# Expert outputs scattered with addition into four rows per token, in a four-part sequence kernel

## The reference

```
logits = x @ gate_w.T ; scores = softmax(logits)          # 64 experts
topk_w, topk_idx = top_k(scores, 6)                       # six experts per token
# an expert takes its first 64 tokens (CAP); the rest is dropped
g = silu(buf @ w_gate) ; u = buf @ w_up ; d = (g * u) @ w_down
y[t] = sum over the experts that took t of  topk_w * d
y = y + shared feed-forward of x
```

## Time and profile before

| what | value |
|---|---|
| time, median of 3 runs | 695.05 us (693.71 to 695.93) |
| the profiled execution: its time, and its span | 695.07 us, 693.3 us |
| TensorE, VectorE, ScalarE, GpSimd busy | 85%, 74%, 28%, 15% |
| chain of waits by engine | PE 50%, DVE 33%, DMA 6%, issue 4%, ACT 3% |
| HBM read, written | 83.99 MB, 30.15 MB |

### The profile page before, as it was taken

One profiled execution on the slowest core, in us unless ns is written; L12 is line 12 of the kernel. 1 busy time (PEld: TensorE's weight loads), 2 busy tenths in 40 slices (PEclk: granted clock), 3 DMA queues, 4 the chain that ended last, 5 costly groups with the idle time before them and its releaser, 6 DMA issues.

```text
span 693.3 us, 7285 instructions
## 1 busy us (share of the span) xinstructions
PE 589.8 (85%) x2297; PEld 334.7 (48%) x2297; DVE 514.0 (74%) x1126; ACT 192.2 (28%) x375; POOL 106.4 (15%) x120
## 2 busy tenths in 40 slices
PE   7569999789998859987889958949599799999865
PEld 6444565435555346543455513534287344444454
DVE  7989888068895859999689996899978355555355
ACT  1112231136432344322543305413110223323000
POOL 2022020300002000020000030000000456664200
PEclk9889999899999959999799977979899999999999
DMA  7960000419102291010750014993071299996497
GB/s 278 405 208 25 16 32 0 134 66 352 43 0 69 93 353 51 23 38 1 282 182 24 1 38 154 348 333 129 0 251 38 77 330 367 373 374 240 178 413 296
DMA packets 50036, 114.62 MB, mean 165 GB/s; under 512 B 6096, under 2 KB 32464, under 8 KB 49488
## 3 DMA queue, kind: packets, MB, share of 16 engines
q1 hardware_dynamic: 42064, 94.36, 38.0%
q0 software_dynamic: 5632, 17.70, 7.3%
q10 hardware_dynamic: 2304, 2.10, 0.9%
HBM read 83.99 MB, written 30.15 MB: 165 GB/s over the span
## 4 chain that ended last, share of the span: by engine, by line
PE 50%; DVE 33%; DMA 6%; issue 4%; ACT 3%; SPq 2%; POOL 1%; DVEq 0%; POOLq 0%; ACTq 0%
PE gate_ps L712 7%; DVE scan_area L1315 7%; PE gate_ps L841 6%; PE up_ps L712 6%; PE misc_ps L729 5%; DMA bc<-part_rows 4%; DVE scan_area L1311 3%; DVE scan_area L1318 3%; PE turn_ps L652 3%; PE ssm_ps L671 3%; PE ssm_ps L761 3%; PE ssm_ps L859 3%; PE misc_ps L812 3%; PE misc_ps L859 3%; SPq L563 2%
## 5 line engine op out<-in xcount | busy, mean ns | idle before, releaser
L1315 DVE TENSOR_TENSOR_SCAN scan_area<-scan_area 128x1024 f32<-128x1024 f32 x32 | 73.3, 2292 | 4.4 <-ACT scan_area L999 0.9
L712 PE MATMUL gate_ps<-big,front_area 128*128 x144 | 74.8, 645 | 1.4 <-ACT front_area L899 1.4
L761 PE MATMUL ssm_ps<-scan_area,ident 128*128 128x512 f32 x128 | 63.5, 629 | 12.6 <-DVE scan_area L1318 11.9
L712 PE MATMUL up_ps<-big,front_area 128*128 x144 | 70.1, 610 | 0.0
L729 PE MATMUL misc_ps<-big,front_area 128*128 x288 | 65.6, 381 | 4.2 <-ACT front_area L899 3.8
L729 PEld LDWEIGHTS misc_ps<-big,front_area 128*128 128x128 f32 x288 | 54.3, 190 | 18.3 <-issue 11.7
L935 ACT ACTIVATE sig<-gate_ps 128x512 f32<-128x512 f32 (+1 forms) x48 | 28.5, 595 | 105.2 <-PE up_ps L712 65.9
L671 PE MATMUL ssm_ps<-zeros,ident 128*128 128x256 f32 x156 | 42.1, 427 | 15.9 <-ACT front_area L899 12.9
L999 ACT ACTIVATE scan_area<-scan_area,a_col 128x511 f32<-128x511 f32 x64 | 42.2, 714 | 39.8 <-DVE scan_area L1315 35.8
L610 POOL DMA_INDIRECT front_area<-ysorted_dram,slot_idx x16 | 18.5, 1155 | 188.0 <-DMA ysorted_dram<-front_area 184.4
L712 PEld LDWEIGHTS up_ps<-big,front_area 128*128 128x128 f32 x144 | 29.0, 201 | 37.9 <-issue 37.9
(11 more groups left out here) (236 smaller groups left out, 904.9 us busy)
## 6 DMA issues: line engine op xcount, KB each, us to landing
bc<-bc_dram SPq DMA_DIRECT2D x4, 4096.0 KB, 13.3
part_rows<-zeros SPq DMA_DIRECT2D x16, 768.0 KB, 15.8
big<-in_wgu SPq DMA_DIRECT2D x15, 704.0 KB
front_area<-in_wgu SPq DMA_DIRECT2D x9, 704.0 KB
big<-part_rows SPq DMA_DIRECT2D x8, 768.0 KB, 9.6
scan_area<-in_wgu SPq DMA_DIRECT2D x6, 704.0 KB
big<-in_wd SPq DMA_DIRECT2D x15, 256.0 KB
front_area<-part_rows SPq DMA_DIRECT2D x5, 768.0 KB, 21.2
```

What stands on the lines that cost most here:

```text
L712: mm = pe.matmul(bank[:], xs_t[:, k, j, :], gu0[:, expert_of[b, j], k, g, half * 512:(half + 1) * 512], start=(k == 0), stop=(k == K - 1))
L761: mm = pe.matmul(ssm_ps[:], ident[:], hs[:, g % HS_RING, n, :], start=False, stop=(g % PER_CHUNK == PER_CHUNK - 1 and n == GROUP - 1))
L1315: nc.vector.tensor_tensor_scan(buf.rearrange(flat), d_a[:, g % 2, :, :].rearrange(flat), buf.rearrange(flat), 0.0, ALU.mult, ALU.add).then ...
```

## The change

A scatter now adds to the rows that it hits. A token has four rows in place of six (of eight): the row is 4 x token + (which expert of the pair) + 2 x (pair number mod 2). Several experts of one token so add into the same row. The two halves of one scatter never meet in a row, and neither do neighbouring pairs; pair p and pair p-2 may, and so scatter p waits until scatter p-2 has landed. Since no rank within the token is needed any more, `places` loses the comparison, the scan and the two operations behind it, and has two operations instead, one per half. In `tables` the two copies into `idx_put` become additions of the row's offset, and `idx_get` gets one operation more, which limits the row numbers of empty slots to the end of a smaller `table`. The reads at the end, the clears and the sums shrink to four rows.

```diff
-PER_TOKEN = 8
-TABLE_ROWS = N + EMPTY // PER_TOKEN
-PART_ROWS = PER_TOKEN * N + EMPTY
+PER_TOKEN = 4
+SETS = PER_TOKEN // 2
+EMPTY_STEP = CAP + PER_TOKEN
+TABLE_ROWS = N + P
+PART_ROWS = PER_TOKEN * N + E * EMPTY_STEP
...
-        placed = marked[:].rearrange("p j e -> p (j e)")[:, 0:J * E]
+        placed = att_s[:].rearrange("p r n -> p (r n)")[:, 0:J * E]
...
-        part_size = TOPK * D
+        part_size = PER_TOKEN * D
...
-                                 zeros[:, 0:D].unsqueeze(1).broadcast_to([P, TOPK, D])).then_inc(parts_clear, 16)
+                                 zeros[:, 0:D].unsqueeze(1).broadcast_to([P, PER_TOKEN, D])).then_inc(parts_clear, 16)
...
+                                             (sum_no[:], [[0, PAIRS // SETS], [2, SETS]], 0, 0)):
...
             for p in range(PAIRS):
                 pool.wait_ge(yo_halves, 2 * (p + 1))
+                if p >= SETS:
+                    pool.wait_ge(rows_put[(p - SETS) % YO_RING], 16 * ((p - SETS) // YO_RING + 1))
                 pool.indirect_dma_start(part_rows, bass.IndirectOffsetOnAxis(idx_put[:, p:p + 1], 0),
-                                        yo[:, p % YO_RING, :], None).then_inc(rows_put[p % YO_RING], 16)
+                                        yo[:, p % YO_RING, :], None, compute_op=ALU.add).then_inc(rows_put[p % YO_RING], 16)
...
-                for k in range(TOPK):
+                for k in range(PER_TOKEN):
                     mm = pe.matmul(sum_ps[i], ident[:], parts[i][:, k * D:(k + 1) * D],
...
-                ts(chosen[:], marked[:, :, 0:E], -3.0, None, ALU.is_equal).then_inc(s, 1)
-                nc.vector.tensor_tensor_scan(nth..., flat, flat, 0.0, ALU.add, ALU.max)
-                stt(out=nth[:], in0=nth[:], scalar=-1.0, in1=wide(tok_value[:, bass.ds(b * J, J)], E), ...)
-                tt(placed.rearrange("p (q h e) -> p h q e", q=2, h=2), nth..., chosen..., ALU.mult)
+                by_half = placed.rearrange("p (q h e) -> p h q e", q=2, h=2)
+                for h in range(2):
+                    at = b * J + 2 * h
+                    stt(out=by_half[:, h, :, :], in0=marked[:, 2 * h:2 * h + 2, 0:E], scalar=-3.0,
+                        in1=wide(tok_value[:, at:at + 2], E), op0=ALU.is_equal, op1=ALU.mult).then_inc(s, 1)
...
-                    nc.vector.tensor_copy(idx_put[rows, :], by_pair[rows, :, e]).then_inc(ids_steps, 1)
+                    stt(out=idx_put[rows, :], in0=by_pair[rows, :, e], scalar=float(e), in1=sum_no[rows, :],
+                        op0=ALU.add, op1=ALU.add).then_inc(ids_steps, 1)
...
-                ts(idx_get, idx_put, 3, None, ALU.logical_shift_right).then_inc(ids_steps, 1)
+                ts(idx_get.bitcast(I32), idx_put.bitcast(I32), float(PER_TOKEN * TABLE_ROWS - 1), None, ALU.min
+                   ).then_inc(ids_steps, 1)
+                ts(idx_get, idx_get, 2, None, ALU.logical_shift_right).then_inc(ids_steps, 1)
...
-                tt(part[:, 0:D], part[:, 0:D], part[:, D:2 * D], ALU.add).then_inc(part_steps, 1)
-                tt(xt, xt, part[:, 2 * D:3 * D], ALU.add).then_inc(part_steps, 1)
-                tt(xt, xt, part[:, 0:D], ALU.add).then_inc(out_ready, 1)
+                tt(xt, xt, part[:, 0:D], ALU.add).then_inc(part_steps, 1)
+                tt(xt, xt, part[:, D:2 * D], ALU.add).then_inc(out_ready, 1)
```

More of the change, by code:

```diff
@@ L80 @@
 GT = 4
-TOP = 2 * J + 6
+TOP = 2 * J + 4
 ROUNDS = CAP // 8
@@ L143, in build @@
         slot_no = sb("slot_no", [E, CAP])
+        sum_no = sb("sum_no", [P, PAIRS])
         zeros = sb("zeros", [P, XW])
@@ L286, in build @@
         part_rows = nc.dram_tensor("part_rows", (PART_ROWS, D), F32).ap()
-        part_of = part_rows[0:PER_TOKEN * N, :].rearrange("(i p r) d -> i p (r d)", p=P, r=PER_TOKEN)[:, :, D:D + part_size]
+        part_of = part_rows[0:PER_TOKEN * N, :].rearrange("(i p r) d -> i p (r d)", p=P, r=PER_TOKEN)
         x_loaded = [sem(f"x_loaded{b}") for b in range(B)]
@@ L524, in ssm_exp @@
                 for j in range(J):
-                    sp.dma_start(part_of[b * J + j].rearrange("p (r d) -> p r d", r=TOPK),
-                                 zeros[:, 0:D].unsqueeze(1).broadcast_to([P, TOPK, D])).then_inc(parts_clear, 16)
+                    sp.dma_start(part_of[b * J + j].rearrange("p (r d) -> p r d", r=PER_TOKEN),
+                                 zeros[:, 0:D].unsqueeze(1).broadcast_to([P, PER_TOKEN, D])).then_inc(parts_clear, 16)
             def weights(p):
@@ L550, in weights_more @@
                     weights(p)
-            sp.wait_ge(pool_consts, 12)
+            sp.wait_ge(pool_consts, 13)
             run(sp, dict(ffn_load=ffn_load, ffn_out=ffn_out, ssm_proj=ssm_proj, ssm_exp=ssm_exp, places=places,
@@ L579, in _ @@
                                              (last_slot[:], [[-P, J]], SLOTS - 1, -1),
-                                             (tok_value[:], [[-PER_TOKEN * L, B], [TOPK - PER_TOKEN * P, J]],
+                                             (tok_value[:], [[-PER_TOKEN * L, B], [-PER_TOKEN * P, J]],
                                               PER_TOKEN * N, -PER_TOKEN),
@@ L584, in _ @@
                                              (counts_down[:], [[-P, J * (B - 1)]], L * (B - 1), 0),
-                                             (slot_no[:], [[1, CAP]], 0, CAP)):
+                                             (slot_no[:], [[1, CAP]], 0, EMPTY_STEP),
+                                             (sum_no[:], [[0, PAIRS // SETS], [2, SETS]], 0, 0)):
                 nc.gpsimd.iota(dst, pattern, base=base, channel_multiplier=mult,
@@ L623, in tables @@
             def tables(b, _):
-                pool.wait_ge(ids_steps, 6)
+                pool.wait_ge(ids_steps, 7)
                 pool.wait_ge(scratch_clear, 16)
@@ L666, in awake @@
                 if b == 0:
-                    pe.wait_ge(pool_consts, 12)
+                    pe.wait_ge(pool_consts, 13)
                 else:
@@ L884, in _ @@
                     pe.wait_ge(last_added, 2)
-                for k in range(TOPK):
+                for k in range(PER_TOKEN):
                     mm = pe.matmul(sum_ps[i], ident[:], parts[i][:, k * D:(k + 1) * D],
-                                   start=(k == 0), stop=(k == TOPK - 1))
+                                   start=(k == 0), stop=(k == PER_TOKEN - 1))
                 mm.then_inc(parts_summed, 1)
@@ L1106, in attn_in @@
                 if b == 0:
-                    dve.wait_ge(pool_consts, 12)
+                    dve.wait_ge(pool_consts, 13)
                 norm(0, b, xn_a[b])
@@ L1473, in _ @@
                 tt(part[:, 0:half], part[:, 0:half], part[:, half:2 * half], ALU.add).then_inc(part_steps, 1)
-                dve.wait_ge(part_steps, 3 * (i // 2) + 1)
-                tt(part[:, 0:D], part[:, 0:D], part[:, D:2 * D], ALU.add).then_inc(part_steps, 1)
-                tt(xt, xt, part[:, 2 * D:3 * D], ALU.add).then_inc(part_steps, 1)
-                dve.wait_ge(part_steps, 3 * (i // 2) + 3)
-                tt(xt, xt, part[:, 0:D], ALU.add).then_inc(out_ready, 1)
+                dve.wait_ge(part_steps, 2 * (i // 2) + 1)
+                tt(xt, xt, part[:, 0:D], ALU.add).then_inc(part_steps, 1)
+                dve.wait_ge(part_steps, 2 * (i // 2) + 2)
+                tt(xt, xt, part[:, D:2 * D], ALU.add).then_inc(out_ready, 1)
                 dve.wait_ge(parts_summed, i // 2 + 1)
```

4 lines of the change are left out of this document (1 added, 3 removed).

## The result

| | before | after |
|---|---|---|
| time, median | 695.02 us (693.71 to 695.93) | 700.96 us (699.27 to 702.4) |
| ratio of after to before | | 1.0088, 95% interval 1.0063 to 1.0112 |
| span of the profiled execution, granted clock | 693.3 us, 0.934 | 699.2 us, 0.910 |
| start of the first scatter | 556.54 | 553.31 |
| first to last start of a scatter | 91.96 | 110.79 |

The account below looks back on a forecast made before the run. It took placing stages on the chain, TensorE without idle time in the expert loop beside full DMA queues, and a DMA-bound end. 695.07 - 4.05 - 10.05 - 0.61 + 5.1 + 2.0 gave 687.5 us; range 683 to 693, 8 in 10 680.5 to 706.

Parts of the forecast that it names:

- The adding scatter, as a wait: Expert loop and its end: waiting for scatter p-2 costs 0 in the loop, 2.0 us at the last landing.
- The margin: Expert loop: the wait for scatter p-2 is met early, with 3.5 us to spare even after another 1.5 us.
- The point from which the rival decides: Expert loop: landing time of an adding scatter, 6.16 us, below which waiting for scatter p-2 costs nothing.
- The wait for scatter p-2 becomes the bound (slower): Rival, GpSimd ahead of each scatter: two pairs can't be shorter than one landing, so the loop grows; chance 0.17.
- L = 8: Rival's case of an adding scatter landing after 8 us: cost 26.7 + 5.6 us, time 712.7 us.
- Placing stages: Batches 0, 1 and 2: two operations for four save 1.35 us each on the chain, 4.05 us; batch 3 nothing.
- Final reads and last sums: End of the kernel: fewer bytes read save 10.05 us, shorter VectorE sums behind the last tile 0.61 us.
- The adding scatter, as DMA work: Expert loop queues: 27 scatters at 0.366 us extra delay the weights 9.9 us, less 4.8 slack, costing 5.1 us.
- GpSimd's issue: Expert loop: a longer scatter instruction on GpSimd costs 0, with 0.53 us of room in a 3.08 us pair.
- The rival of a longer issue: GpSimd's issue passes 1.5 us and binds 24 pairs: some 694 to 700 us; chance 0.17 shared with heavier DMA work.
- The last landing: End of the loop: the last scatter waits for an earlier one and lands at 652.9 instead of 650.9, +2.0 us.

Follow-up runs that it names:

- tail4: Kernel before with only four of its six rows of a token read and summed at the end; 688.74 us, its before 697.2.
- beforeadd: Kernel before with adding scatters in its own six-row layout and no wait; 701.41 us, its before 697.39, ratio 1.0066.

## Why the prediction was wrong

The step that failed is "The adding scatter, as a wait": "One issued at 599.69 has landed by 602.36 in the full stream (its 48 packets are all within the window to 602.36), 2.67 us." The 48 packets are there, but they are not its own: they are 32 of 4 KB, 15 of a few bytes and one of a gather. A scatter's 32 packets of 4 KB come once in 3.08 us, so nearly every window of 3 us holds a set. Those that start from 601.03 to 602.04 us belong to the scatter issued at 596.61, whose semaphore has its last recorded update at 602.90; those of the one issued at 599.69 start from 604.24 to 604.99, and its semaphore's last recorded update is at 606.02, after 6.3 us. Window 604.2:605.1 of the kernel before:

```profile
q0 software_dynamic: 42, 0.13, 37.7%
```

The rest follows from this:

- The margin. It was put at 6.16 - 2.67 = 3.5 us; with 6.3 us and the 0.75 us from landing to start, it was -0.9 before any addition. The point from which the rival decides was put at L = 6.16 without the 0.75 us; it is 5.4.
- The rival "The wait for scatter p-2 becomes the bound (slower)" came true, at the place and by the sign given, with a chance of 0.17. At its L = 8 it gave 712.7 us, too much: it let 29 intervals grow, but landings are long only until the weights' stream ends, 18 or 19 scatters in, and the loop grew by 18.8 us instead of 26.7, the last landing by 1.4 instead of 5.6. Its counter-argument ("the measured 2.67 us leaves much room") was the misreading again.
- An adding landing takes 3.8 us in queues without weights and about 8 in full ones, a plain one 2.4 and 6.3; the one read in an empty stretch, 2.40 us, said nothing of the full one. The Trainium skill, DMA: Bandwidth & Descriptors, section "Latency and other measured facts", has an access to memory take ten times as long at high load as in the mean; the trace agrees in direction, with a factor of 2 to 2.6 for the whole landing.

The other steps:

- Placing stages: -4.05 forecast; 1.45 us a stage, 4.35 in three, measured, and 3.7 to 3.9 by undoing them. Right. (The first scatter starts only 3.2 us earlier: between the two profiled executions 3.3 us were lost ahead of the first such stage, where TensorE's granted clock is lower in one stretch, 0.6 instead of 0.8 at 35 to 52 us, and 2.2 more were won between that stage and the first scatter. No run ties these two to the change.)
- Final reads and last sums: -10.66 forecast, -11.1 between the traces, -10.0 in the trace of tail4. Right.
- "The adding scatter, as DMA work": +5.1 forecast, 0 measured. In beforeadd the weights came 4.3 us later for 27 scatters, 0.16 us each instead of 0.366, and the slack of 4.8 us took it; in the changed kernel their last packet moves at 631.8 us, earlier than before. The rule of the Trainium skill cited there (Collectives: The Full Stack, "The bandwidth ceiling: the fold count and why AG ≠ RS ≠ AR"), half a copy's rate, agrees with the packets' own times beside the weights (128 x 103 ns against 32 x 182 ns, a factor of 2.3), but it was not the rate that was paid for; the landing was.
- GpSimd's issue: cost 0 was forecast, "so there is 0.53 us of room"; it grew by 0.60 us, so a pair is 3.18 instead of 3.08 us where nothing waits. 1.1 us in the loop, by beforeadd. The rival of a longer issue had the right place and a small size.
- The last landing: +2.0 forecast, +1.4 measured.

The placing stages, the end and the last landing were sized well; what failed lies in the loop. With the loop at +18.8 in place of +5.1 and the landing at 1.4, the sum of the same terms is 695.07 - 4.35 - 11.1 + 18.8 + 1.4 = 699.8, against 700.96 measured.

## What to carry to other kernels

When a change makes an instruction wait for a DMA that nobody waited for before, measure that DMA's time to landing in the stretch where the wait will stand, under its traffic, by issue and landing of the same one; packets in a window are not an identity. Add the time from landing to the next start, and compare with the distance in time. If it is close, move the wait further back (three sets instead of two, with bf16 rows, or four with fp32 rows took the whole wait out of the loop here) rather than make the transfer faster.

## What the runs showed of the hardware

- An indirect scatter with addition costs GpSimd 1.58 us instead of 0.98 to issue, and moves as 128 packets of 1 KB instead of 32 of 4 KB. A packet takes 103 ns in the mean beside the weights and 142 in quiet queues, where the plain one's takes 182 and 179. The changed kernel's DMA view of 638.7:641.8, with one scatter and one gather, beside 45 packets and 12.2% in the earlier trace rows:

```profile
DMA packets 175, 0.28 MB, mean 92 GB/s; under 512 B 26, under 2 KB 143, under 8 KB 175
...
q0 software_dynamic: 175, 0.28, 54.6%
...
part_rows<-bc,att_s POOLq DMA_INDIRECT x1, 3.9
```

- It lands after 3.8 us with quiet queues and after 7 to 9 with full ones; a plain one after 2.4 and 6.3. With its bytes halved it stays at 6.6 to 8.9 with full queues.
- From a landing to the start of a waiting indirect DMA on GpSimd 0.75 us pass where the other wait stood right ahead, and 0.27 where a gather was issued between the two waits.
